# Attention stage of a transformer layer: gathering the halves of the diagonal score tiles that survive a merge

## The reference

```python
q, k, v = ...                      # 32 query heads, 8 key/value heads, 8 features each
scores = einsum('bhqd,bhkd->bhqk', q, k) / sqrt(8)
amask = where((j >= i - 128) & (j < i), -1e10, 0)   # the 128 keys before a query are masked OUT
out = softmax(scores + amask) @ v
x = x + out @ wo
x = x + moe(layernorm(x))          # 8 routed experts, top 2, and 2 shared ones
```

## Time and profile before

| | |
|---|---|
| median of 3 runs | 999.13 us (998.54 to 999.97) |
| the profiled execution | 1002.57 us, span 1000.8 us |
| attention groups | from about 71 to 530 us of the span |
| mean granted TensorE clock | 0.976 of full |

### The profile page before, as it was taken

How to read it: one execution, slowest core, us unless ns; L and a number is a source line. 1 busy time by engine, 2 the same in 40 slices (tenths; PEclk the granted TensorE clock), 3 DMA queues, 4 the chain that set the end, 5 groups by cost and what they waited for, 6 DMA issues and landing times.

```text
span 1000.8 us, 23830 instructions
## 1 busy us (share of the span) xinstructions
PE 896.4 (90%) x7905; PEld 551.8 (55%) x7906; DVE 462.5 (46%) x808; ACT 592.5 (59%) x792; POOL 322.8 (32%) x422
## 2 busy tenths in 40 slices
PE   3839999999999999999986999999888999999994
PEld 1413333333333333333335898988777788888884
DVE  5734344443444344434344747475872333333332
ACT  2639999999999999999992333333211222222221
POOL 8005344434444444434330000000011454444442
PEclk9979999999999999999997999999999899999998
DMA  4354544455555444422012102501006882655621
GB/s 137 97 170 164 197 145 152 137 184 186 188 186 196 169 152 175 129 80 81 25 54 69 42 23 70 192 0 42 1 6 247 255 249 46 199 139 135 167 37 22
DMA packets 42089, 123.74 MB, mean 124 GB/s; under 512 B 7616, under 2 KB 23104, under 8 KB 35904
## 3 DMA queue, kind: packets, MB, share of 16 engines
q1 hardware_dynamic: 31568, 110.78, 32.0%
q0 software_dynamic: 7008, 9.70, 5.6%
q10 hardware_dynamic: 3472, 2.76, 0.8%
HBM read 74.06 MB, written 49.15 MB: 123 GB/s over the span
## 4 chain that ended last, share of the span: by engine, by line
PE 57%; ACT 19%; DVE 8%; issue 7%; DMA 4%; SPq 2%; POOL 1%; POOLq 1%; DVEq 0%; ACTq 0%
ACT arena L812 16%; PE ps L1591 12%; PE ps L1406 10%; PE ps L1423 10%; PE ps L1519 9%; PE ps L1610 6%; PE ps L1532 4%; PE ps L1601 2%; DMA wr_all<-w_scr 2%; PE ps L1470 1%; ACT arena L808 1%; DVE ps L973 1%; PE ps L1488 1%; SPq L434 1%; POOL arena L669 1%
## 5 line engine op out<-in xcount | busy, mean ns | idle before, releaser
L812 ACT ACTIVATE arena<-ps 128x1024 f32<-128x1024 f32 x384 | 360.8, 1045 | 5.1 <-PE ps L1423 0.4
L669 POOL TENSOR_SCALAR_AFFINE_SELECT arena<-arena 128x512 f32<-128x512 f32 x240 | 194.4, 819 | 309.6 <-PE ps L1423 175.6
L1423 PE MATMUL ps<-arena 128*32 128x256 f32 x4096 | 279.2, 386 | 1.6 <-POOL arena L669 0.5
L1406 PE MATMUL ps<-arena 64*128 64x512 bf16 x1024 | 176.2, 387 | 43.4 <-ACT arena L812 15.5
L1423 PEld LDWEIGHTS ps<-arena 128*32 128x32 f32 x4096 | 104.8, 109 | 120.5 <-issue 67.1
L1591 PE MATMUL ps<-wr_all,x2T 128*128 x648 | 147.6, 369 | 7.3 <-issue 4.3
L1406 PEld LDWEIGHTS ps<-arena 64*128 64x128 bf16 x1024 | 44.8, 93 | 197.8 <-ACT arena L812 128.1
L1591 PEld LDWEIGHTS ps<-wr_all,x2T 128*128 128x128 f32 x648 | 107.4, 192 | 30.3 <-issue 15.6
L1519 PE MATMUL ps<-x2T,wr_all 128*128 (+1 forms) x480 | 118.5, 399 | 2.4 <-DVE arena L1095 2.4
L1519 PEld LDWEIGHTS ps<-x2T,wr_all 128*128 128x128 f32 x480 | 90.1, 193 | 20.7 <-DVE arena L1095 2.8
L703 POOL COPY now_from<-slot_from 128x1 int32 (+1 forms) x36 | 8.3, 230 | 263.0 <-issue 244.3
(11 more groups left out here) (179 smaller groups left out, 795.8 us busy)
## 6 DMA issues: line engine op xcount, KB each, us to landing
w_scr<-wr_all SPq DMA_DIRECT2D x24, 1280.0 KB, 5.0
wr_all<-w_scr SPq DMA_DIRECT2D x24, 1280.0 KB, 5.6
raw<-w_experts SPq DMA_DIRECT2D x24, 640.0 KB, 9.2
arena<-q_scr SPq DMA_DIRECT2D x64, 64.0 KB
o_scr<-arena SPq DMA_DIRECT2D x128, 32.0 KB, 1.7
arena<-o_scr SPq DMA_DIRECT2D x16, 256.0 KB, 4.0
raw<-w_shared SPq DMA_DIRECT2D x6, 640.0 KB, 5.6
q_scr<-parts SPq DMA_DIRECT2D x8, 384.0 KB, 2.7
```

Of the source, the lines that this page charges most:

```text
L669: nc.gpsimd.affine_select(out=dst, in_=src, compare_op=ALU.is_ge if own else ALU.is_gt, fill=0.0, base=0, pattern=[[0, REP], [-1 if own el ...
L812: nc.scalar.activation(prob[:, SLOT[k], :, :].rearrange("p h q -> p (h q)"), score.rearrange("p b x -> p (b x)"), ACT.Exp, scale=SCALE).th ...
L1406: last = nc.tensor.matmul(ps[:, 2 * BUF[k] + half, :], kst[r0:r0 + HALF, s, kt * P:(kt + 1) * P], qst[r0:r0 + HALF, s, :, a * QW:(a + 1) * ...
L1423: last = nc.tensor.matmul(ps[32 * h:32 * h + 32, 6 + qc, a % 2 * QW:(a % 2 + 1) * QW], vst[:, s, kt, :], prob[:, SLOT[k], h, :], start=(no ...
```

## The change

What it does:

- Units are no longer the items that ScalarE works through. 29 exponentials a group (`EXPS`) are of three kinds. *Plain* (21): a whole unit without masked halves. *Merged* (4, one a query pair): the two halves that need a merge, the left half of `below` and the right half of `own`, are scored side by side into one pair of banks. *Mixed* (4): the two halves that need none, the right half of `below` and the left half of `own`, side by side. For pair 0 the merged one holds the left half of the source and the right half of `own`, and the mixed one is a half.
- Each of them is one exponential, with an output strided over two slots (`probs_of`); the exponential by bank is gone.
- A merged or mixed score unit is two pieces x two row tiles, 4 matmuls of 256 columns.
- The source tile is no longer scored into a buffer of its own. Its two head halves go one after the other into one bank (`X_BANK`: bank 7, for pair 3 bank 6), an accumulator bank that is idle at that time: `source(.., 0)` after the merged scores, `source(.., 1)` one turn later, once the first copy has read the bank. Each is one matmul of 512 columns (256 for pair 0).
- VectorE merges bank by bank: two predicated copies a pair with one mask tile `keep` for both sides, 512 elements a partition each (256 for pair 0).
- A merged score unit is issued one place ahead of its exponential (`issue_order`).
- Each turn has one value unit, three of them two (`value_order`), where before half the turns had none. 29 turns a group in place of 32.
- Slots are fixed: six for masked units, alternating between query pairs, six for plain ones.
- The weight splits move: part 0 after the merge of pair 2 (ahead of the copy-out of bank 6), part 1 after that of pair 3, both of the same group. SyncE's order follows, part by part.

```diff
+MIXED_AT, MERGED_AT = (6, 11, 15, 24), (7, 10, 16, 23)
+X_BANK = (7, 7, 7, 6)
...
+def issue_order():
+    order = list(range(NEXP))
+    for j in MERGED_AT:
+        order[j - 1], order[j] = j, j - 1
+    return order
...
+    turns = {2: (plain[0],), 3: (plain[1],), 4: (plain[2],), 5: (plain[3],), 6: (plain[4],), 7: (plain[5],),
+             8: (plain[8],), 9: (plain[9],), 10: (source_of(0),), 11: (own_of(0),), 12: (plain[12],),
+             13: (below_of(1),), 14: (plain[13], plain[14]), 15: (source_of(1),), 16: (own_of(1),), 17: (plain[17],),
+             18: (plain[18],), 19: (below_of(2),), 20: (plain[19],), 21: (source_of(2), own_of(2)), 22: (plain[20],),
+             23: (plain[21],), 24: (plain[22],), 25: (plain[25],), 26: (below_of(3), plain[26]), 27: (plain[27],),
+             28: (source_of(3),), 29: (own_of(3),), 30: (plain[28],)}
...
             def group_io(n, s, split, following, more):
+                for p in range(2):
+                    if split:
+                        store_split(n, p)
+                    if following:
+                        load_next(n + 1, p)
+                    if p == 0:
+                        store_acc(n, 0)
                 if more:
-                    sp.wait_ge(s_ready, n * UNITS + UNITS)
+                    sp.wait_ge(s_ready, n * NEXP + NEXP)
                     load_pair(n + 2, s)
                 store_acc(n, 1)
...
+                for e, (kind, a, kt) in enumerate(EXPS):
+                    for k in slots_written(e):
+                        back, v = tenant_before(k)
+                        act.wait_ge(p_free, n * UNITS + (UNITS * (1 - back) + VALUE_NO[v] + 1))
+                    if kind == MERGED:
+                        act.wait_ge(merged, n * NMERGE + (2 * a + 2))
+                    else:
+                        act.wait_ge(s_ready, n * NEXP + (ISSUE_NO[e] + 1))
...
+            def merge_pair(g, a):
+                sides = slice(0 if a else 1, 2)
                 for bank in range(2):
+                    wait_apart(dve, x_ready, g * NMERGE + (2 * a + bank + 1))
+                    into = ps[:, 2 * BUF[MERGED_AT[a]] + bank, :].rearrange("p (h s q) -> p h s q", h=2, s=2)[:, :, sides, :]
+                    source = ps[:, X_BANK[a], :].rearrange("p (h s q) -> p h s q", h=2, s=2)[:, :, sides, :]
+                    mask = keep[:, sides, :].bitcast(I32).unsqueeze(1).to_broadcast([P, 2, sides.stop - sides.start, P])
+                    nc.vector.copy_predicated(into, mask, source).then_inc(merged, 1)
...
             def group(g, s, more):
                 merge_pair(g, 1)
-                split_part(g, 1)
                 merge_pair(g, 2)
+                split_part(g, 0)
                 acc_out(g, 0)
                 merge_pair(g, 3)
-                if following:
-                    split_part(g + 1, 0)
-                merge_first(g + 1)
+                split_part(g, 1)
                 acc_out(g, 1)
+                merge_pair(g + 1, 0)
...
+                pe.wait_ge(s_free, n * NEXP + (i + 1))
+                e = ISSUE[i]
+                kind, a, kt = EXPS[e]
+                left, right = 2 * a, 2 * a + 1
+                pieces = {PLAIN: [(0, left, 2, kt)],
+                          MERGED: [(0, left, 1, left - 1 if a else left), (1, right, 1, right)],
+                          MIXED: [(0, right, 1, left - 1)] * (a > 0) + [(1, left, 1, right)]}[kind]
+                for piece in pieces:
+                    for half in range(2):
+                        last = score(s, 2 * BUF[e] + half, half, *piece)
                 last.then_inc(s_ready, 1)
+                if kind == MERGED:
+                    source(n, s, a, 0)
+                if e + 1 in MERGED_AT:
+                    source(n, s, MERGED_AT.index(e + 1), 1)
+
+            def source(n, s, a, half):
+                if half:
+                    pe.wait_ge(merged, n * NMERGE + (2 * a + 1))
+                elif a == 0:
+                    pe.wait_ge(acc_free, n * QC + 2)
+                elif X_BANK[a] == X_BANK[a - 1]:
+                    pe.wait_ge(merged, n * NMERGE + 2 * a)
+                else:
+                    pe.wait_ge(acc_free, n * QC + 3)
+                piece = (0, 2 * a, 2, 2 * a) if a else (1, 1, 1, 0)
+                score(s, X_BANK[a], half, *piece).then_inc(x_ready, 1)
```

More of the change, by code:

```diff
@@ L64, in slot_of, with plain_of, unit @@
     return (e + 2) % WSLOTS
[L67 to L73 removed]
+PLAIN, MIXED, MERGED = "plain", "mixed", "merged"
+BELOW, SOURCE, OWN = range(3)
+def plain_of(a):
+    return [kt for kt in range(KT) if kt not in (2 * a - 1, 2 * a, 2 * a + 1)]
+def unit(a, kt):
+    return a * KT + kt
+UNIT = [(a, kt) for a in range(QP) for kt in range(KT)]
@@ L96, with exponentials @@
-NMERGE = max(MERGED.values())
-def buffers():
-    buf, turn = [], [0, 1, 2]
-    for k in range(UNITS):
-        if k % KT == 3 and k // KT in (1, 3):
-            i, j = (k - 3) % BUFS, (k - 2) % BUFS
-            turn[i], turn[j] = turn[j], turn[i]
-        buf.append(turn[k % BUFS])
+    return unit(a, 2 * a + 1)
+MIXED_AT, MERGED_AT = (6, 11, 15, 24), (7, 10, 16, 23)
+X_BANK = (7, 7, 7, 6)
+def exponentials():
+    plain = iter([(PLAIN, a, kt) for a in range(QP) for kt in plain_of(a)])
+    special = {j: (kind, a, None) for kind, where in ((MIXED, MIXED_AT), (MERGED, MERGED_AT)) for a, j in enumerate(where)}
+    return [special[j] if j in special else next(plain) for j in range(len(special) + sum(len(plain_of(a)) for a in range(QP)))]
@@ L143 @@
 MASK_OPS = 3 + 4 * (QP - 1)
+NMERGE = 2 * QP
 def masks_before(k):
```

248 lines of the change are left out of this document (113 added, 135 removed).

## The result

The changed kernel takes 1013.03 us (median of 4 runs, 1012.3 to 1013.31) against 999.55 us (4 runs, 998.54 to 999.99) for the kernel before: 1.0135 times as long, 95% interval 1.0118 to 1.0153. The change makes the kernel 13.5 us slower.

The account below looks back on a forecast made before the run. ScalarE bounds the kernel before; after the change TensorE does, 24.6 + 3.1 - 0.8 + 1.5 + 0.9 = 29.3 us a group against 28.4. Over 15 periods that is +13.5 on 999.1: 1012 us, range 982 to 1030.

Parts of the forecast that it names:

- its own chain: Merge steps timed from T, the end of the exponential four before a merged one: VectorE's second copy runs T + 2.09 to 2.79.
- Alternation, +3.1: TensorE switching between score and value tilings: 13 more alternations a group at 0.24 us each, +3.1 us.
- the upper bound: Longest time taken for a run of one value unit on TensorE, 0.60 us; using it would add 0.8 a group.
- the first rival: ScalarE stays the bound because single runs alternate more cheaply on TensorE: period 27.1, 980 us, faster; chance 0.24.
- Score columns, -0.8: TensorE's scores: 28.5 units' worth a group against 32, at 0.22 us each, -0.8 us.
- The bound of +0.7: Allowance on TensorE: loading the second piece of a gathered score unit may cost another 0.10, seven times a group.
- Sources, +1.5: Source matmuls on TensorE: seven half-filled ones of full width's worth a group, a unit of 0.22 us each, +1.5 us.
- The wait for the bank, +0.9: TensorE's second source awaits the first copy: 0.2 idle plus 0.1 for uncovered weights, three times a group, +0.9 us.
- The sum of 29.3: TensorE's time a group after the change, 24.6 + 3.1 - 0.8 + 1.5 + 0.9 us, against 28.4 before.
- VectorE, GpSimd and SyncE at nothing: Copies, moved weight splits, masks and reordered loads cost nothing; if the cover went, TensorE would stand up to 0.5 a group.
- The last group's 1.76 us: Pair 3's copies behind two reciprocals hold TensorE up about as long as the 1.81 ScalarE lost before.
- three scores of lookahead: Scoring ahead of ScalarE's exponentials doesn't help, for over a group TensorE needs 29.3 us and ScalarE 27.1.

Follow-up runs that it names:

- e6: The kernel before with its value units spread over 28 turns a group in place of 16, nothing else: 1027.61 us, ratio 1.0289.
- e1: The changed kernel with four more value units joined to a neighbour's turn, 25 value runs a group in place of 29: 1006.9 us, ratio 1.0079.
- e8: The changed kernel with each source matmul issued twice in a row into the same bank: 1039.9 us, ratio 1.041.
- e4: The changed kernel without the second source matmul of each pair, so half the merged scores are wrong: 991.96 us, ratio 0.9919.
- e7: The changed kernel with the first weight split put back ahead of pair 2's merge on VectorE: 1014.37 us, ratio 1.0152.
- e1 to e3: Three plans of the changed kernel with 25, 18 and 16 value runs a group in place of 29: 1006.9, 1013.93 and 1000.64 us.
- e5: The changed kernel with 20 value runs a group, double ones kept out of the merged units' turns and those just ahead: 991.24 us, ratio 0.9912.
- e9: e5 with three of its double value turns moved one turn later, right ahead of the turns that score merged units: 1007.65 us, ratio 1.008.

## Why the prediction was right, and where it was not

The forecast was 1012 us and slower; 1013.03 was measured, and the mechanism is the one it named.

*ScalarE's gain was real and worthless.* Its work in a group fell by about 0.2 us (27.22 to 27.06), and its idle time rose by more. Idle grew from 1.15 to 2.04 us a group, where about 2.5 was forecast; and it does not all wait for scores, as the forecast had it, but for scores and for copies by halves. The half exponentials stand 29.11 apart, where 29.3 was forecast, and VectorE's second copy starts 1.29 after its first: the forecast said about 1.4, while its own chain (T + 0.81 and T + 2.09) makes it 1.28.

*Alternation, +3.1.* Right. A value run of one takes 0.57 to the next scores and carries the label "issue" in a plain turn, in the kernel after and in e6; 0.57 was the value taken, 0.60 the upper bound. The gap from the last value weights to the next score weights is 0.41 in the earlier trace rows after runs of two and three, and 0.41 after a run of one. So the first rival (980 us) fell on the row that it had named. With it, for this pair of tilings, fell the free alternation that the prediction drew from the rule of "TensorE: Matmul & The Clock Gate", Part 2, in the Trainium skill, that one matmul's drain overlaps the next one's fill. What the Trainium skill says in "TensorEngine Tiling (Array Packing)", Key Properties, that a change of mode drains the array, agrees with these rows; they show the gap of 0.41 and not what the array does in it. e1 shows the price at work: 0.96 for four.

*Score columns, -0.8, and their second pieces.* Right, with the second piece of a gathered unit at nothing: a turn of four score matmuls of 256 columns takes 0.89 (316.20 to 317.09), as one of two with 512. The bound of +0.7 was not needed.

*Sources, +1.5.* Right: 0.226 each by e8, where 0.22 was taken. They overlap nothing.

*The wait for the bank, +0.9.* This term was too large. The distance from the first source's end to the second's start is 0.90 as worked out (the copy starts at 314.56, 0.15 after that end, and the second source's load stands at 315.31). The prediction's own figures leave 0.90 + 0.07 - 0.57 - 0.22 = 0.18 of it idle, and 0.18 is what e4 gives and what the rows show (314.34 to 315.31 is 0.97, less 0.57 and 0.22). It had rounded that to 0.2 and added 0.1 for a weight load that nothing covers, and no such 0.1 shows. So 0.54 in place of 0.9. The sum of 29.3 also owes something to rounding: its terms unrounded make 24.64 + 3.12 - 0.77 + 1.54 + 0.9 = 29.43, and with 0.54 and sources at 0.226 they make 29.11, the measured period.

*The total.* The period grew by 0.72 and not 0.9, and 15 x 0.72 = 10.8. The start and the end of the stage added 2, which the sum did not have, and 0.8 of the 13.5 is not accounted for. Two misses of 2 to 3 us in opposite directions are why 1012 (its sum says 1012.6) is closer than its terms deserve: the mechanism is right, the last few us are luck.

*VectorE, GpSimd and SyncE at nothing.* Right for VectorE's moved split (e7: 0.02 us). TensorE never waits for a mask in the group shown: of the four masks after pair 2 the next value unit needs two, done at 326.05, and its weights load at 327.58, 0.53 after the turn's first scores as in the other turns with a first source, though the label there names GpSimd. The last group's 1.76 us was forecast.

*What the prediction missed* did not change its number but changes its lesson. It said that three scores of lookahead don't help, because TensorE needs 29.3 and ScalarE 27.1: two bounds, and the larger wins. There is a third between them. The unit issued out of order leaves the exponential in front of a merged one with next to no slack, and lateness of TensorE at those three turns goes straight through to ScalarE. Hidden in the changed kernel, where TensorE is full anyway, it showed as soon as TensorE was relieved: 28.2 to 28.9 in e1 to e3 where 26.0 to 28.2 was TensorE's sum. e5 and e9 settle it. In most groups e5 still loses 0.44 us at these places (0.65 in the one shown); a plan that gets that back, too, was not tried.

## What to carry to other kernels

When an engine works through two kinds of items that need two modes, count its runs, not only its items: here each extra pair of switches cost 0.24 us beside a unit of 0.22 to 0.43, and an even spread of the values, which looks kindest to the consumer, cost 28 us in the kernel before (e6, waits for merges included) and 22 us in the changed one against the best order found. Taking work off the bound engine pays only as far as the next bound, so sum the other engine's program order turn by turn before the edit; the saving here came only after the values had been paired again at the right turns (20 runs, 991 us). Pairing alone did not give it: 18 runs in the wrong turns took 1014 us. And where an item is issued out of order, look for the neighbour whose slack paid for it, and keep the long turns away from it.

## What was unexpected of the hardware

The 128x1280 subtraction of the weight split on VectorE (L1045) takes 1.49 us after and 1.80 before, and GpSimd's masks take 0.72 against 0.84 on average, both at the same shapes. The traces show what goes with it. A mask lasts 0.63 us when no subtraction runs beside it and 1.0 to 1.9 when one does; before, two masks stand beside each subtraction (59 of 240 are long), after, one does (31 of 240). The subtraction lasts 1.80 where masks run beside it for its whole length or nearly (29 of 30 before) and 1.49 where they do for 1.2 us or less (all 30 after). Moving the split on VectorE (e7) changes neither figure; no run took the masks away, so that they slow each other stays an inference from the overlap. Striding the exponential's output over two slots costs nothing: 1023 ns for the merged and mixed ones against 1052 and 1045 for the plain ones, after and before.
